# One-core fused block: output product over rounded halves from the third batch, first layer norm by aggregations

## The chip, the cores and the metric

The kernel runs on one core of a Trainium2 chip. The metric is device time in microseconds (us) of one execution. The time before is 390.41 us, the median of 3 runs (390.02 to 390.94).

## The reference

16 batches of a 512 x 256 activation pass through a state-space layer and a channel mixer, each behind a modulated layer norm. Cut to what matters:

```
h = layernorm(x) * (1 + ca) + sa
u, gate = split(h @ W_in.T)
decay = exp(-min(softplus(u @ W_dt.T + b_dt), 10) * rate)
state[t] = decay[t] * state[t-1] + (1 - decay[t]) * (u @ W_state.T)[t]
z = (state @ W_C.T) * silu(gate) + h * D
x1 = x + ga * (z @ W_out.T)              # the output product
h2 = layernorm(x1) * (1 + cb) + sb
xr, xk = mixes of h2 and h2 one token earlier
x2 = x1 + gb * sigmoid(xr @ W_r) * (relu(xk @ W_k)^2 @ W_v)
```

## The kernel before, in words

Every engine has a hand-written list of instructions, one block of code for each engine, and all of them loop over the same STEPS (20 of them, s = 0 to 19). In step s four batches are at work: a = s (first layer norm), b = s-1 (state-space layer and output product), c = s-2 (second layer norm and the mixes), d = s-3 (channel mixer and output). Nothing reorders the instructions: what stands late in an engine's list waits for what stands before it, and semaphores tie the lists together.

Channels lie on the partitions, in 2 halves of 128, and the 512 tokens of a batch along the free axis, so a tile `x[:, i]` is 128 x 512. Most products are done in float32r over rounded halves: ScalarE (ACT) copies x into `x_hi` (rounded), GpSimd (POOL) subtracts it to get `x_lo` (helper `low_part`, L665), and TensorE (PE) multiplies `x_hi` by `w_hi` and `w_lo` and `x_lo` by `w_hi`. That is so for `h` (front and gate products), `xk`, `xr` and `k_act`. Two products are in plain float32: `state` with `w_y` (L320), and the output product, `z` with `w_late` at OUT. `half` (L207) issues the matmuls of one input half: two, one for each output half.

The end of a PE step reads: second norm's transposes, `k_hi` products, transposes of `xn1`, `k_lo` half 0, `z` half 0, `k_lo` half 1, `z` half 1 (which raises `o_ps`). The next step opens with the K product, `xk_hi` half 0 with `wl_hi` and `wl_lo`, and waits for `xk_hi`, both `xk` and both `xr`. Then come `xk_hi` half 1, four `h_hi` products, `xk_lo` half 0, four `h_hi`, `xk_lo` half 1, two `h_lo`, and the transposes of `x1` (L290).

ACT ends a step with `r_gate` (tanh, L465) and four `prev` (L392), and opens the next with `xk_hi` half 0 (L400), `h` (L407), `xk_hi` half 1 (L410), `h` (L412), `h_hi` (L415). VectorE (DVE) computes `z` (L604), the mixes `xk`, `xr`, `xr`, `xk` (L550; the second pair waits for the fourth `prev`), the first norm's statistics two batches ahead (L489), the gated value (L624), the first norm's `mean_variance` (five operations on 128 x 4, L496 to L505), `x2` (L631), `x1` (L637, waits for `o_ps`). `x1` reads the output product from PSUM, and the second norm and the residual need it. POOL runs `xk_lo` twice, `h_lo` twice, `xr_lo`, `rstd2` (L698), `prev`'s first column, `xr_lo`, the first norm's scale (`ln1_scale`, L672 and L674), `k_lo` twice.

Of the kernel before, what the change touches and what calls it, by code (L numbers as in the profile page):

```python
# [26 lines left out]
def adaln_block(nc, x_tok_d, x_ch_d, w_d, wmod_d, c_d, cols_d, ident_d, out_d):  # L27
# [6 lines left out]
    with ExitStack() as ctx:  # L34
        def sb(name, shape, dt=F32):
            return ctx.enter_context(nc.sbuf_tensor(name, shape, dt))

        def sem(name):
            return ctx.enter_context(nc.semaphore(name))

        def sems(name, n=CH):
            return [sem(f"{name}{i}") for i in range(n)]
# [9 lines left out]
        w_front = sb("w_front", [P, CH, 2 * NS])  # L52
        wf_hi = sb("wf_hi", [P, CH, 2 * NS + C], F32R)
        wf_lo = sb("wf_lo", [P, CH, 2 * NS + C], F32R)
        wl_hi = sb("wl_hi", [P, CH, 3 * C], F32R)
        wl_lo = sb("wl_lo", [P, CH, 3 * C], F32R)
        ident = sb("ident", [P, P])
        cols = sb("cols", [P, 8])
        c_sb = sb("c_sb", [P, CH * NB])
# [16 lines left out]
        x_ch = sb("x_ch", [P, 2, CH, T])  # L76
        x1 = sb("x1", [P, 3, CH, T])
        stats1 = sb("stats1", [P, 2, TT, 6])
        mv1 = sb("mv1", [P, 2, 5, TT])
        rstd1 = sb("rstd1", [P, 2, TT])  # L80
        shift1 = sb("shift1", [P, 2, TT])
        xn1 = sb("xn1", [P, TT, C])
# [50 lines left out]

        xn1a_ok, h_ok, hhi_ok, e_ok, l_ok, decay_ok = sem("xn1a_ok"), sem("h_ok"), sem("hhi_ok"), sem("e_ok"), sem("l_ok"), sem("decay_ok")
        silu_ok, tanh_ok, khi_ok, relu_ok, kact_ok = sem("silu_ok"), sem("tanh_ok"), sem("khi_ok"), sem("relu_ok"), sem("kact_ok")
        prev_ok, xkhi_ok, xrhi_ok = sems("prev_ok"), sems("xkhi_ok"), sems("xrhi_ok")

        st1_ok, halves1_ok, spread1_ok, mv1_ok, xn1b_ok = sem("st1_ok"), sem("halves1_ok"), sem("spread1_ok"), sem("mv1_ok"), sem("xn1b_ok")
        st2_ok, halves2_ok, spread2_ok, mv2_ok = sem("st2_ok"), sem("halves2_ok"), sem("spread2_ok"), sem("mv2_ok")
        xn2a_ok, xn2b_ok = sem("xn2a_ok"), sem("xn2b_ok")  # L140
        clip_ok, drive_ok, state_ok, yg_ok, rv_ok = sem("clip_ok"), sem("drive_ok"), sem("state_ok"), sem("yg_ok"), sem("rv_ok")
        z_ok, x1_ok, xk_ok, xr_ok, x2_ok = sems("z_ok"), sems("x1_ok"), sems("xk_ok"), sems("xr_ok"), sems("x2_ok")

        rstd1_ok, shift1_ok, rstd2_ok, first_ok = sem("rstd1_ok"), sem("shift1_ok"), sem("rstd2_ok"), sem("first_ok")
        hlo_ok, xklo_ok, xrlo_ok, klo_ok = sems("hlo_ok"), sems("xklo_ok"), sems("xrlo_ok"), sems("klo_ok")

        def col(j):
            return cols[:, j:j + 1]
# [54 lines left out]
        def _(pe):  # L203
# [43 lines left out]
            for s in STEPS:  # L247
                a, b, c, d = s, s - 1, s - 2, s - 3
                if live(d):
                    if d == 0:  # L250
                        pe.wait_ge(wl_lo_ok, 3)
                    pe.wait_ge(xkhi_ok[0], d + 1)
                    for x_done in (*xk_ok, *xr_ok):
                        pe.wait_ge(x_done, d + 1)
                    half(k_out, wl_hi, MIX_K, xk_hi, 0, first=True)
                    half(k_out, wl_lo, MIX_K, xk_hi, 0)
                if live(d):
                    pe.wait_ge(xkhi_ok[1], d + 1)
# [118 lines left out]

        @block.scalar
        def _(act):
# [14 lines left out]

            for s in STEPS:
                a, b, c, d = s, s - 1, s - 2, s - 3
                if live(d):
                    act.wait_ge(xk_ok[0], d + 1)
                    before(act, k_ps, d)
                    nc.scalar.copy(xk_hi[:, 0], xk[:, 0]).then_inc(xkhi_ok[0], 1)  # L400
# [56 lines left out]
                if b == 0:  # L457
                    act.wait_ge(s_wl, 16)
                    for at in (MIX_K, MIX_R, MIX_V):
                        nc.scalar.copy(wl_hi[:, :, at:at + C], w_late[:, :, at:at + C]).then_inc(wl_hi_ok, 1)  # L460
                if live(d):
                    nc.scalar.activation(k_act[:], k_act[:], ACT.Square).then_inc(kact_ok, 1)  # L462
                    act.wait_ge(r_ps, d + 1)
                    before(act, rv_ok, d)
                    nc.scalar.activation(r_gate[:], ps_r[:], ACT.Tanh, scale=0.5).then_inc(tanh_ok, 1)  # L465
                if live(c):
                    if c == 0:
                        act.wait_ge(mix_ok, 1)
                    act.wait_ge(t3_ps, c + 1)
                    before(act, xk_ok[0], c)  # L470
                    previous(KEY, 0, c)
                    before(act, xr_ok[0], c)
                    previous(REC, 0, c).then_inc(prev_ok[0], 1)
                    before(act, xr_ok[1], c)
                    previous(REC, 1, c)
                    before(act, xk_ok[1], c)
                    previous(KEY, 1, c).then_inc(prev_ok[1], 1)

        @block.vector
        def _(dve):  # L480
# [8 lines left out]
                    last = nc.vector.bn_stats(st[:, t, :], x[:, t, :])  # L489
                last.then_inc(st_ok, 1)  # L490

            def mean_variance(st, mv, st_ok, halves_ok, spread_ok, mv_ok, k, negative=False):
# [6 lines left out]
                if negative:  # L499
                    nc.vector.scalar_tensor_tensor(mv[:, 0, :], mv[:, 2, :], 0.5, st[:, :, 1], ALU.mult, ALU.subtract)  # L500
                else:
                    nc.vector.scalar_tensor_tensor(mv[:, 0, :], mv[:, 2, :], -0.5, st[:, :, 1], ALU.mult, ALU.add)
# [79 lines left out]
            for s in STEPS:  # L582
# [78 lines left out]
        def _(pool):  # L661
# [22 lines left out]
            for s in STEPS:  # L684
# [64 lines left out]
```

## Time and profile before

| | before |
|---|---|
| time, median of 3 | 390.41 us (390.02 to 390.94) |
| the profiled execution's own time | 390.1 us |
| its span | 388.3 us, granted TensorE clock 0.996 |
| PE busy | 369.3 us (95%) |
| weight loads (PEld) busy | 265.3 us (68%) |
| DVE busy | 317.1 us (82%) |
| ACT busy | 288.6 us (74%) |
| POOL busy | 201.8 us (52%) |

Times are us from the span's start. A row of a timeline reads: start, duration (of the group, where x2 or more stand at its end), engine, line, operation, tiles, and in brackets the idle time before it and what ended it. A float32 matmul of 128 x 512 shows as two matmul records with a weight load each, a float32r one as one. PEld is the weight load, which runs ahead of its matmul. POOL's queue and the DMAs keep up; neither stands in the way in the stretches discussed.

### The profile page before, as it was taken

The page shows a single profiled execution, that of the slowest core. Times are in us where ns is not written, and L with a number is a line of the kernel's source. Part 1 is how long each engine was busy: PE and PEld are TensorE (multiplying, and loading weights), DVE is VectorE, ACT ScalarE, POOL GpSimd, SP SyncE. Part 2 cuts the span into 40 slices and gives each one's busy share as a digit, 9 for nine tenths or more (in the row PEclk, how much of TensorE's full clock was granted, in tenths as well). Part 3 has the DMA queues.
Part 4 walks back from the last instruction along what each step waited for, and adds up shares of the span by engine and source line. Part 5 has one row for each costly group of instructions (what it writes and reads, how often), then busy time and mean ns, then how long its engine had stood idle before and what let it go on. Part 6 is the DMA issues. An engine that isn't in the chain of part 4 may idle for free.

```text
span 388.3 us, 5293 instructions
## 1 busy us (share of the span) xinstructions
PE 369.3 (95%) x1624; PEld 265.3 (68%) x1627; DVE 317.1 (82%) x653; ACT 288.6 (74%) x375; POOL 201.8 (52%) x198
## 2 busy tenths in 40 slices
PE   8998899999999999999999999999999999999773
PEld 4766487676777677676767767676767767676651
DVE  3787987989889797988979798888979787768552
ACT  4467678687887878689687868888787878967471
POOL 2053355666364556656454566645455663635552
PEclk9999999999999999999999999999999999999998
DMA  8921111130403131040313113040302020000111
GB/s 283 394 77 54 54 57 54 56 110 0 164 0 108 55 104 60 12 152 0 118 47 108 56 56 107 3 159 3 111 0 87 24 92 17 23 32 0 57 54 54
DMA packets 18604, 29.13 MB, mean 75 GB/s; under 512 B 1168, under 2 KB 9616, under 8 KB 18448
## 3 DMA queue, kind: packets, MB, share of 16 engines
q1 hardware_dynamic: 18144, 28.71, 21.4%
q8 instruction: 13, 0.21, 0.2%
q10 hardware_dynamic: 432, 0.09, 0.1%
q14 instruction: 15, 0.12, 0.1%
HBM read 20.40 MB, written 8.39 MB: 74 GB/s over the span
## 4 chain that ended last, share of the span: by engine, by line
issue 49%; POOL 37%; PE 7%; DVE 3%; ACT 2%; POOLq 1%; DVEq 0%; ACTq 0%
POOL xr_lo L665 10%; POOL xk_lo L665 10%; POOL k_lo L665 6%; POOL h_lo L665 5%; POOL rstd L672 3%; PE slot L207 2%; PE slot L228 2%; PE slot L221 1%; DVE stats L489 1%; PE slot L320 1%; POOLq L24 1%; POOL prev L703 1%; PE slot L214 1%; ACT prev L392 1%; DVE state L587 1%
## 5 line engine op out<-in xcount | busy, mean ns | idle before, releaser
L665 POOL TENSOR_TENSOR xk_lo<-xk,xk_hi 128x512 fp32r<-128x512 f32 x32 | 40.9, 1279 | 52.7 <-ACT xk_hi L400 47.1
L207 PE MATMUL slot<-z,w_in 128*128 128x512 f32 x128 | 59.8, 592 | 0.0
L698 POOL TENSOR_TENSOR rstd<-mv,half_neg 128x4 f32<-128x4 f32 x16 | 16.1, 1007 | 76.5 <-DVE mv L505 76.5
L665 POOL TENSOR_TENSOR k_lo<-k_act,k_hi 128x512 fp32r<-128x512 f32 x32 | 40.6, 1291 | 20.7 <-ACT k_act L462 20.7
L392 ACT ACTIVATE prev<-slot,mod,mix_prev 128x512 f32<-128x512 f32 x64 | 44.5, 784 | 2.8 <-PE slot L214 2.8
L207 PE MATMUL slot<-h_hi,wf_hi 128*128 128x512 f32 x128 | 46.0, 400 | 0.4 <-ACT h_hi L415 0.4
L207 PE MATMUL slot<-h_hi,wf_lo 128*128 128x512 f32 x128 | 45.1, 393 | 0.0
L665 POOL TENSOR_TENSOR h_lo<-h,h_hi 128x512 fp32r<-128x512 f32 x30 | 38.3, 1298 | 9.6 <-ACT h_hi L415 9.6
L427 ACT ACTIVATE dt<-slot,cols 128x512 f32<-128x512 f32 x16 | 11.0, 688 | 41.5 <-PE slot L207 41.5
L665 POOL TENSOR_TENSOR xr_lo<-xr,xr_hi 128x512 fp32r<-128x512 f32 x32 | 41.5, 1299 | 0.0
L550 DVE SCALAR_TENSOR_TENSOR xk<-slot,mix_new,prev 128x512 f32<-128x512 f32 x32 | 23.9, 747 | 18.8 <-issue 18.8
L214 PE MATMUL slot<-ident,xn 128*128 128x128 f32 x256 | 35.7, 273 | 2.8 <-DVE xn L526 2.1
L207 PE MATMUL slot<-h_lo,wf_hi 128*128 128x512 f32 x128 | 37.4, 395 | 0.0
L214 PEld LDWEIGHTS slot<-ident,xn 128*128 128x128 f32 x256 | 30.4, 140 | 10.1 <-DVE xn L526 2.8
L207 PEld LDWEIGHTS slot<-z,w_in 128*128 128x128 f32 x128 | 24.0, 189 | 18.8 <-issue 16.3
L320 PE MATMUL slot<-state,w_in 128*128 128x512 f32 x64 | 30.2, 594 | 2.5 <-DVE state L587 2.5
L526 DVE TENSOR_SCALAR xn<-slot,mv,rstd 128x256 f32<-128x256 f32 x64 | 30.1, 534 | 1.1 <-POOL rstd L698 1.1
L599 DVE TENSOR_TENSOR slot<-silu,slot 128x1024 f32<-128x1024 f32 x16 | 19.7, 1229 | 13.5 <-PE slot L320 13.5
L465 ACT ACTIVATE r_gate<-slot 128x1024 f32<-128x1024 f32 x16 | 16.4, 1028 | 18.6 <-PE slot L207 18.6
L207 PEld LDWEIGHTS slot<-h_hi,wf_hi 128*128 128x128 f32 x128 | 24.0, 188 | 6.7 <-issue 0.9
L207 PE MATMUL slot<-xk_hi,wl_hi 128*128 128x512 f32 x64 | 26.2, 491 | 2.2 <-DVE xk L550 2.2
L207 PEld LDWEIGHTS slot<-h_hi,wf_lo 128*128 128x128 f32 x128 | 24.2, 189 | 5.9 <-issue 0.2
(99 smaller groups left out, 900.4 us busy)
## 6 DMA issues: line engine op xcount, KB each, us to landing
x_tok<-x_tok_in SPq DMA_DIRECT2D x16, 512.0 KB, 3.5
x_ch<-x_ch_in SPq DMA_DIRECT2D x16, 512.0 KB, 3.9
x_out<-wmod SPq DMA_DIRECT2D x15, 512.0 KB, 3.0
wmod<-wmod_in SPq DMA_DIRECT2D x1, 1024.0 KB, 10.1
w_in<-weights_in SPq DMA_DIRECT2D x1, 1024.0 KB, 11.5
w_in<-weights_in SPq DMA_DIRECT2D x1, 768.0 KB, 5.5
wmod<-wmod_in SPq DMA_DIRECT2D x1, 512.0 KB, 6.4
x_out<-wmod SPq DMA_DIRECT2D x2, 256.0 KB, 2.2
```

Of the source, the lines that this page charges most:

```text
L207: ins = nc.tensor.matmul(out, w[:, c, at + d * P:at + (d + 1) * P], x[:, c, :], start=first, stop=last)
L214: last = nc.tensor.transpose(out[:, c, t * P:(t + 1) * P], x[:, t, c * P:(c + 1) * P], ident[:])
L320: last = nc.tensor.matmul(ps_y[:, i, :], w_y[:, i * P:(i + 1) * P], state[:], start=True, stop=True)
L392: return nc.scalar.activation(prev[:, mix, i, 1:T + 1], ps_n[:, i, :], ACT.Identity, bias=mod_at(SHIFT2 + i, k), scale=mix_prev[:, mix, i, ...
L427: nc.scalar.activation(dt[:], ps_front[:, 0, :], ACT.Exp, bias=col(B_DT)).then_inc(e_ok, 1)
L465: nc.scalar.activation(r_gate[:], ps_r[:], ACT.Tanh, scale=0.5).then_inc(tanh_ok, 1)
L526: last = nc.vector.tensor_scalar(xn2[:, t, :], ps_x1[:, t, :], mv2[:, k % 2, 0, t:t + 1], rstd2[:, k % 2, t:t + 1], ALU.subtract, ALU.mult)
L550: nc.vector.scalar_tensor_tensor(x[:, i, :], ps_n[:, i, :], mix_now[:, mix, i, k:k + 1], prev[:, mix, i, 0:T], ALU.mult, ALU.add).then_inc ...
L599: nc.vector.tensor_tensor(ps_y[:], silu[:], ps_y[:], ALU.mult).then_inc(yg_ok, 1)
L665: nc.gpsimd.tensor_tensor(lo, x, hi.bitcast(F32), ALU.subtract).then_inc(done, 1)
L672: nc.gpsimd.tensor_tensor(rstd1[:, k % 2], mv1[:, k % 2, 1, :], half_neg[:], ALU.pow).then_inc(rstd1_ok, 1)
L698: nc.gpsimd.tensor_tensor(rstd2[:, c % 2], mv2[:, c % 2, 1, :], half_neg[:], ALU.pow).then_inc(rstd2_ok, 1)
```

## The change

The output product of batches 2 to 15 (`split(k)`) goes over rounded halves: ACT copies z into z_hi (half 0 between the second and the third `prev`, half 1 at the head of the next step), POOL makes z_lo after `k_lo`, and PE multiplies z_hi by the halves of W_out where z stood, and z_lo inside the K product of the next step, which is where `o_ps` is raised now. Batches 0 and 1 stay in float32. ACT and POOL split W_out once, in step 2. The first norm's mean and variance are made by one aggregation per token tile, four in all, and POOL negates the mean and adds epsilon.

```diff
+        WHOLE = 2
+        def split(k):
+            return WHOLE <= k < NB
 # PE, head of a step
                     half(k_out, wl_hi, MIX_K, xk_hi, 0, first=True)
                     half(k_out, wl_lo, MIX_K, xk_hi, 0)
+                if split(c):
+                    pe.wait_ge(zlo_ok[0], c - WHOLE + 1)
+                    half(o_out, wl_hi, OUT, z_lo, 0)
                 if live(d):
                     pe.wait_ge(xkhi_ok[1], d + 1)
                     half(k_out, wl_hi, MIX_K, xk_hi, 1)
                     half(k_out, wl_lo, MIX_K, xk_hi, 1)
+                if split(c):
+                    pe.wait_ge(zlo_ok[1], c - WHOLE + 1)
+                    half(o_out, wl_hi, OUT, z_lo, 1, last=True).then_inc(o_ps, 1)
 # PE, end of a step
-                    pe.wait_ge(z_ok[0], b + 1)
                     before(pe, tanh_ok, d + 1 if live(d) else 0)
-                    half(o_out, w_late, OUT, z, 0, first=True)
+                    if split(b):
...
+                        pe.wait_ge(zhi_ok[0], b - WHOLE + 1)
+                        half(o_out, wl_hi, OUT, z_hi, 0, first=True)
+                        half(o_out, wl_lo, OUT, z_hi, 0)
+                    else:
+                        pe.wait_ge(z_ok[0], b + 1)
+                        half(o_out, w_late, OUT, z, 0, first=True)
                 if live(d):
                     pe.wait_ge(klo_ok[1], d + 1)
                     half(v_out, wl_hi, MIX_V, k_lo, 1, last=True).then_inc(v_ps, 1)
-                if live(b):
+                if split(b):
+                    pe.wait_ge(zhi_ok[1], b - WHOLE + 1)
+                    half(o_out, wl_hi, OUT, z_hi, 1)
+                    half(o_out, wl_lo, OUT, z_hi, 1)
+                elif live(b):
                     pe.wait_ge(z_ok[1], b + 1)
                     half(o_out, w_late, OUT, z, 1, last=True).then_inc(o_ps, 1)
 # ACT
+                if split(c):
+                    act.wait_ge(z_ok[1], c + 1)
+                    nc.scalar.copy(z_hi[:, 1], z[:, 1]).then_inc(zhi_ok[1], 1)
...
+                if b == 1:
+                    nc.scalar.copy(wl_hi[:, :, OUT:OUT + C], w_late[:, :, OUT:OUT + C]).then_inc(wl_hi_ok, 1)
...
                     previous(REC, 0, c).then_inc(prev_ok[0], 1)
+                if split(b):
+                    act.wait_ge(z_ok[0], b + 1)
+                    before(act, o_ps, b)
+                    nc.scalar.copy(z_hi[:, 0], z[:, 0]).then_inc(zhi_ok[0], 1)
+                if live(c):
                     before(act, xr_ok[1], c)
                     previous(REC, 1, c)
 # DVE
-                mean_variance(stats1[:, k % 2], mv1[:, k % 2], st1_ok, halves1_ok, spread1_ok, mv1_ok, k, negative=True)
+                dve.wait_ge(st1_ok, k + 1)
+                for t in range(TT):
+                    last = nc.vector.bn_aggr(mv1[:, k % 2, t, :], stats1[:, k % 2, t, :])
+                last.then_inc(mv1_ok, 1)
...
-                        before(dve, o_ps, b)
+                        if split(b - 1):
+                            dve.wait_ge(zlo_ok[i], b - WHOLE)
+                        else:
+                            before(dve, o_ps, b)
 # POOL
-                nc.gpsimd.tensor_tensor(rstd1[:, k % 2], mv1[:, k % 2, 1, :], half_neg[:], ALU.pow).then_inc(rstd1_ok, 1)
+                nc.gpsimd.tensor_scalar(spread1[:, k % 2, 0, :], mv1[:, k % 2, :, 0], -1.0, None, ALU.mult)
+                nc.gpsimd.tensor_scalar(spread1[:, k % 2, 1, :], mv1[:, k % 2, :, 1], EPS, None, ALU.add).then_inc(spread1_ok, 1)
+                pool.wait_ge(spread1_ok, k + 1)
+                nc.gpsimd.tensor_tensor(rstd1[:, k % 2], spread1[:, k % 2, 1, :], half_neg[:], ALU.pow).then_inc(rstd1_ok, 1)
...
+                if split(b):
+                    for i in range(CH):
+                        pool.wait_ge(zhi_ok[i], b - WHOLE + 1)
+                        pool.wait_ge(o_ps, b)
+                        nc.gpsimd.tensor_tensor(z_lo[:, i], z[:, i], z_hi[:, i].bitcast(F32), ALU.subtract).then_inc(zlo_ok[i], 1)
```

Line numbers in the changed kernel are higher (L207 is L216 there). On PE, at the turn of a step, before:

```order
L207 MATMUL slot<-k_lo,wl_hi 128x512 x2
L207 MATMUL slot<-z,w_in 128x512 x2
L207 MATMUL slot<-xk_hi,wl_hi 128x512 x2
L207 MATMUL slot<-xk_hi,wl_lo 128x512 x2
L207 MATMUL slot<-xk_hi,wl_hi 128x512 x2
L207 MATMUL slot<-xk_hi,wl_lo 128x512 x2
L207 MATMUL slot<-h_hi,wf_hi 128x512
```

The same place in the changed kernel:

```order
L216 MATMUL slot<-k_lo,wl_hi 128x512 x2
L216 MATMUL slot<-z_hi,wl_hi 128x512 x2
L216 MATMUL slot<-z_hi,wl_lo 128x512 x2
L216 MATMUL slot<-xk_hi,wl_hi 128x512 x2
L216 MATMUL slot<-xk_hi,wl_lo 128x512 x2
L216 MATMUL slot<-z_lo,wl_hi 128x512 x2
L216 MATMUL slot<-xk_hi,wl_hi 128x512 x2
L216 MATMUL slot<-xk_hi,wl_lo 128x512 x2
L216 MATMUL slot<-z_lo,wl_hi 128x512 x2
L216 MATMUL slot<-h_hi,wf_hi 128x512
```

Two float32 matmuls per half became four float32r ones, and two more per half moved into the K product.

On ACT at the same turn, in the changed kernel (before, the four `prev` stood together and `xk_hi` came right after them):

```order
L496 ACTIVATE r_gate<-slot 128x1024
L418 ACTIVATE prev<-slot,mod,mix_prev 128x512 x2
L508 CAST z_hi<-z 128x512
L418 ACTIVATE prev<-slot,mod,mix_prev 128x512 x2
L425 CAST z_hi<-z 128x512
L429 CAST xk_hi<-xk 128x512
L436 ACTIVATE h<-slot,mod 128x512
L439 CAST xk_hi<-xk 128x512
```

One copy stands ahead of the third and fourth `prev`, the other ahead of `xk_hi`, `h` and `h_hi`.

## Rows read from the trace of the kernel before

**Rows 1.** Timeline, PE: first K matmuls of steps 14, 15 and 16.

```profile
292.69 1.03 PE L207 MATMUL slot<-xk_hi,wl_hi 128*128 128x512 f32 x2
...
314.94 1.03 PE L207 MATMUL slot<-xk_hi,wl_hi 128*128 128x512 f32 x2
...
336.69 1.03 PE L207 MATMUL slot<-xk_hi,wl_hi 128*128 128x512 f32 x2
```

**Rows 2.** Waits: engine line <- releaser: us in total, times, longest.

```profile
PE slot L290 <- DVE x L637: 3.2, 11, 0.3
```

**Rows 3.** Timeline, weight loads at the turn of a step.

```profile
199.94 0.42 PEld L207 LDWEIGHTS slot<-z,w_in 128*128 128x128 f32 x2
...
203.65 0.19 PEld L207 LDWEIGHTS slot<-xk_hi,wl_hi 128*128 128x128 f32 x1 [0.24 <-issue]
...
205.71 0.19 PEld L207 LDWEIGHTS slot<-h_hi,wf_hi 128*128 128x128 f32 x1
...
208.50 0.42 PEld L207 LDWEIGHTS slot<-h_lo,wf_hi 128*128 128x128 f32 x2
```

**Rows 4.** Timeline, DVE and POOL: the first norm's small operations, x2, x1.

```profile
204.24 0.16 DVE L496 TENSOR_TENSOR mv<-stats 128x4 f32<-128x4 f32 x1
...
204.39 2.56 POOL L665 TENSOR_TENSOR h_lo<-h,h_hi 128x512 fp32r<-128x512 f32 x2 [0.48 <-ACT h_hi L415]
204.52 1.19 DVE L500 SCALAR_TENSOR_TENSOR mv<-mv,stats 128x4 f32<-128x4 f32 x1
...
206.89 1.40 DVE L631 SCALAR_TENSOR_TENSOR wmod<-slot,mod,x 128x512 f32<-128x512 f32 x2
...
208.21 1.39 DVE L637 SCALAR_TENSOR_TENSOR x<-slot,mod,x_ch 128x512 f32<-128x512 f32 x2
```

**Rows 5.** Timeline, ACT: head of one step, end of it and head of the next.

```profile
200.29 0.64 ACT L400 CAST xk_hi<-xk 128x512 fp32r<-128x512 f32 x1
200.80 0.81 ACT L407 ACTIVATE h<-slot,mod 128x512 f32<-128x512 f32 x1
...
201.94 0.62 ACT L410 CAST xk_hi<-xk 128x512 fp32r<-128x512 f32 x1 [0.32 <-DVE xk L550]
...
203.26 1.05 ACT L415 CAST h_hi<-h 128x1024 fp32r<-128x1024 f32 x1
...
209.40 0.69 ACT L427 ACTIVATE dt<-slot,cols 128x512 f32<-128x512 f32 x1 [2.64 <-PE slot L207]
...
218.98 1.03 ACT L465 ACTIVATE r_gate<-slot 128x1024 f32<-128x1024 f32 x1 [1.11 <-PE slot L207]
...
219.90 2.78 ACT L392 ACTIVATE prev<-slot,mod,mix_prev 128x512 f32<-128x512 f32 x4
...
222.55 0.64 ACT L400 CAST xk_hi<-xk 128x512 fp32r<-128x512 f32 x1
```

**Rows 6.** Timeline, DVE: the mixes of that step.

```profile
221.44 0.75 DVE L550 SCALAR_TENSOR_TENSOR xk<-slot,mix_new,prev 128x512 f32<-128x512 f32 x1 [1.15 <-issue]
...
222.10 1.40 DVE L550 SCALAR_TENSOR_TENSOR xr<-slot,mix_new,prev 128x512 f32<-128x512 f32 x2
...
223.42 0.74 DVE L550 SCALAR_TENSOR_TENSOR xk<-slot,mix_new,prev 128x512 f32<-128x512 f32 x1
```

**Rows 7.** Timeline, steps 16 to 18: prev, x1's transposes, last waits on xn and xk.

```profile
352.41 2.78 ACT L392 ACTIVATE prev<-slot,mod,mix_prev 128x512 f32<-128x512 f32 x4
...
360.62 0.95 PEld L290 LDWEIGHTS slot<-ident,x 128*128 128x128 f32 x8
...
366.26 0.66 PE L214 MATMUL slot<-ident,xn 128*128 128x128 f32 x4 [2.11 <-DVE xn L526]
...
371.87 0.74 DVE L550 SCALAR_TENSOR_TENSOR xk<-slot,mix_new,prev 128x512 f32<-128x512 f32 x1
...
372.79 0.30 PEld L207 LDWEIGHTS slot<-xk_hi,wl_hi 128*128 128x128 f32 x2 [2.61 <-issue]
```

**Rows 8.** Timeline, POOL in step 0: the first norm's shift.

```profile
8.08 0.20 POOL L674 TENSOR_TENSOR shift<-mv,rstd 128x4 f32<-128x4 f32 x1
```

More of the change, by code:

```diff
@@ L54, in adaln_block @@
         wf_lo = sb("wf_lo", [P, CH, 2 * NS + C], F32R)
-        wl_hi = sb("wl_hi", [P, CH, 3 * C], F32R)
-        wl_lo = sb("wl_lo", [P, CH, 3 * C], F32R)
+        wl_hi = sb("wl_hi", [P, CH, 4 * C], F32R)
+        wl_lo = sb("wl_lo", [P, CH, 4 * C], F32R)
         ident = sb("ident", [P, P])
@@ L78, in adaln_block @@
         stats1 = sb("stats1", [P, 2, TT, 6])
-        mv1 = sb("mv1", [P, 2, 5, TT])
+        mv1 = sb("mv1", [P, 2, TT, 2])
+        spread1 = sb("spread1", [P, 2, 2, TT])
         rstd1 = sb("rstd1", [P, 2, TT])
@@ L94, in adaln_block @@
         z = sb("z", [P, CH, T])
+        z_hi = sb("z_hi", [P, CH, T], F32R)
+        z_lo = sb("z_lo", [P, CH, T], F32R)
         prev = sb("prev", [P, 2, CH, T + 1])
@@ L135, in adaln_block @@
         silu_ok, tanh_ok, khi_ok, relu_ok, kact_ok = sem("silu_ok"), sem("tanh_ok"), sem("khi_ok"), sem("relu_ok"), sem("kact_ok")
-        prev_ok, xkhi_ok, xrhi_ok = sems("prev_ok"), sems("xkhi_ok"), sems("xrhi_ok")
-        st1_ok, halves1_ok, spread1_ok, mv1_ok, xn1b_ok = sem("st1_ok"), sem("halves1_ok"), sem("spread1_ok"), sem("mv1_ok"), sem("xn1b_ok")
+        zhi_ok, prev_ok, xkhi_ok, xrhi_ok = sems("zhi_ok"), sems("prev_ok"), sems("xkhi_ok"), sems("xrhi_ok")
+        st1_ok, mv1_ok, xn1b_ok = sem("st1_ok"), sem("mv1_ok"), sem("xn1b_ok")
         st2_ok, halves2_ok, spread2_ok, mv2_ok = sem("st2_ok"), sem("halves2_ok"), sem("spread2_ok"), sem("mv2_ok")
@@ L142, in adaln_block @@
         z_ok, x1_ok, xk_ok, xr_ok, x2_ok = sems("z_ok"), sems("x1_ok"), sems("xk_ok"), sems("xr_ok"), sems("x2_ok")
-        rstd1_ok, shift1_ok, rstd2_ok, first_ok = sem("rstd1_ok"), sem("shift1_ok"), sem("rstd2_ok"), sem("first_ok")
-        hlo_ok, xklo_ok, xrlo_ok, klo_ok = sems("hlo_ok"), sems("xklo_ok"), sems("xrlo_ok"), sems("klo_ok")
+        spread1_ok, rstd1_ok, shift1_ok, rstd2_ok, first_ok = sem("spread1_ok"), sem("rstd1_ok"), sem("shift1_ok"), sem("rstd2_ok"), sem("first_ok")
+        hlo_ok, zlo_ok, xklo_ok, xrlo_ok, klo_ok = sems("hlo_ok"), sems("zlo_ok"), sems("xklo_ok"), sems("xrlo_ok"), sems("klo_ok")
         def col(j):
@@ L367, in _ @@
                         pe.wait_ge(s_wl, 16)
-                    pe.wait_ge(z_ok[0], b + 1)
                     before(pe, tanh_ok, d + 1 if live(d) else 0)
-                    half(o_out, w_late, OUT, z, 0, first=True)
+                    if split(b):
+                        if b == WHOLE:
+                            pe.wait_ge(wl_lo_ok, 4)
+                        pe.wait_ge(zhi_ok[0], b - WHOLE + 1)
[4 more added lines that the diff above has]
+                        half(o_out, w_late, OUT, z, 0, first=True)
                 if live(d):
@@ L490, in statistics, with mean_variance @@
                 last.then_inc(st_ok, 1)
-            def mean_variance(st, mv, st_ok, halves_ok, spread_ok, mv_ok, k, negative=False):
+            def mean_variance(st, mv, st_ok, halves_ok, spread_ok, mv_ok, k):
                 dve.wait_ge(st_ok, k + 1)
@@ L498, in mean_variance @@
                 dve.wait_ge(halves_ok, k + 1)
[L499 to L502, printed above, removed]
+                nc.vector.scalar_tensor_tensor(mv[:, 0, :], mv[:, 2, :], -0.5, st[:, :, 1], ALU.mult, ALU.add)
                 nc.vector.scalar_tensor_tensor(mv[:, 4, :], mv[:, 2, :], 0.25, mv[:, 2, :], ALU.mult, ALU.mult).then_inc(spread_ok, 1)
@@ L671, in ln1_scale @@
                 before(pool, xn1b_ok, k - 1)
-                nc.gpsimd.tensor_tensor(rstd1[:, k % 2], mv1[:, k % 2, 1, :], half_neg[:], ALU.pow).then_inc(rstd1_ok, 1)
+                nc.gpsimd.tensor_scalar(spread1[:, k % 2, 0, :], mv1[:, k % 2, :, 0], -1.0, None, ALU.mult)
+                nc.gpsimd.tensor_scalar(spread1[:, k % 2, 1, :], mv1[:, k % 2, :, 1], EPS, None, ALU.add).then_inc(spread1_ok, 1)
+                pool.wait_ge(spread1_ok, k + 1)
+                nc.gpsimd.tensor_tensor(rstd1[:, k % 2], spread1[:, k % 2, 1, :], half_neg[:], ALU.pow).then_inc(rstd1_ok, 1)
                 pool.wait_ge(rstd1_ok, k + 1)
-                nc.gpsimd.tensor_tensor(shift1[:, k % 2], mv1[:, k % 2, 0, :], rstd1[:, k % 2], ALU.mult).then_inc(shift1_ok, 1)
+                nc.gpsimd.tensor_tensor(shift1[:, k % 2], spread1[:, k % 2, 0, :], rstd1[:, k % 2], ALU.mult).then_inc(shift1_ok, 1)
             def weight_low_part(n, at):
@@ L713, in _ @@
                         weight_low_part(n, at)
+                if b == 1:
+                    weight_low_part(4, OUT)
 def kernel(**inputs):
```

## The prediction

> **What bounds the kernel now.** I read the page first: PE is busy 95% of the span, the others far less, so what counts is PE's list and the few places where it waits. The chain that ended last runs mostly through "issue" and POOL and says little here; the timeline of PE says more. The first K matmuls of steps 14, 15 and 16 stand 22.25 and 21.75 us apart [rows 1]. The two intervals hold the same matmuls; the longer one has a wait of x1's transposes for DVE, which occurs 11 times [rows 2]. The row counts 0.29 us of idleness, but the step is 0.50 us longer: the following loads have lost their lead too. So a step is 21.75 us of pure matmul issue, plus 0.50 in 11 steps. ACT waits for PE before r_gate, 1.11 us [rows 5], and catches up with it every step: a step can be reckoned from r_gate's start to r_gate's start.
>
> Below, times lie in the turn after 218.98; a row from the turn before it is moved by 222.55 - 200.29 = 22.26 us [rows 5].
>
> **PE's work.** A float32 record takes 0.19 + 0.24 = 0.43 us from load to load; in float32r the 12 loads from 205.71 to 208.50 take 0.2325 each [rows 3]. Before, a batch has 8 records (3.44 us); now 12 (2.79). Saved: **0.65 us per batch**, 14 batches. Where the matmul itself is 4 passes to 1, by the Trainium skill's FP8 and Floating Point Precision (TensorE Precision Notes: true FP32 takes four passes through the array), the three products would be 3/4 of 3.44, 2.58, and 0.86 saved. The trace gives the float32r matmul 0.2325 and not 3.44 / 16 = 0.215, and the sum goes by the trace.
>
> **x1's wait.** DVE's first-norm block takes 206.89 - 204.24 = 2.65 us for five operations on 4 columns, since some last 1.19 while POOL runs h_lo [rows 4] and 0.16 otherwise. Four aggregations take its place. No row shows one; the nearest are these: 0.16 with starts 0.08 apart for 4 columns would make 0.4 for the group, four statistics of 256 columns (some 0.35 each) 1.4 at most. I take 0.5, as an aggregation reads 6 columns. x1 ends now 7.71 us after the last xk (from 224.16, which is rows 6, to 208.21 + 1.39 + 22.26 = 231.87); new 7.71 - 2.65 + 0.5 = 5.56 after it. If this beats PE, 11 x 0.50 = **5.5 us** go.
>
> **The new wait, at the K product.** Each of ACT's copies pushes what follows by 0.51 (200.29 to 200.80 [rows 5]). The prevs start 0.665 apart. So z_hi half 0 starts at 221.23, the fourth prev at 222.41 and ends at 223.19. DVE's second xr follows by 0.09 (as 221.44 follows the second prev's end), xk by 0.66, and it ends at 224.68, 0.52 later than now [rows 5, 6]. PE's load follows by 0.18 (372.61 to 372.79 [rows 7]): 224.86. PE would be free for it sooner: first z load 199.94 + 22.26 = 222.20 [rows 3], plus 10 loads of 0.2325, 224.52. It is 0.34 late; after a wait the second load comes 0.30 - 0.19 = 0.11 behind the first [rows 7], which gives 0.12 back. **Loss 0.22 us per turn.** z_hi half 1 ends at 223.69, its load free at 223.59: also late, and covered by the K wait.
>
> Next in line, all from the K load at 224.86:
> - h_hi: ACT's second copy and the later xk_hi move it to an end at 227.13; PE asks for it at 224.86 - 0.12 + 12 x 0.2325 = 227.53. Slack 0.40.
> - POOL has two more subtractions of 1.28 in front of xk_lo and h_lo. z_lo half 1 starts at 223.79, xk_lo end at 227.6, h_lo at 230.1; PE asks at 227.53 + 2.79 = 230.32. **Slack 0.2**, the thinnest.
> - x1: 224.68 + 5.56 = 230.24, o_ps long there (about 228.1); PE asks at 230.32 + 0.465 = 230.79. Slack 0.5; the aggregations may cost up to 1.0.
>
> xr_hi and the table load fall into ACT's 2.6 us wait for dt. POOL's small additions in ln1_scale (2 x 0.20 by the shift's row [rows 8], and a semaphore) lie one step ahead of their use; in step 0 they may cost 0 to 0.5, less what the shorter aggregation gives; I take 0. The split of W_out in step 2 meets idle ACT and POOL.
>
> **The tail.** In step 16 no xn1 transposes stand ahead of z. With prev at 352.41 [rows 7] the same steps give xk's end at 357.21, K load 357.39, z_lo half 1 last load 359.83. What reads a product starts some 0.67 after its last load (208.73, the second of the pair in rows 3, to 209.40 [rows 5]), so o_ps releases x1 at 360.5; it ends at 361.9. Transposes start at 361.95, not 360.62 [rows 7]. PE later idles 2.11 for xn, which comes from x1: the whole **1.33 us** is lost.
>
> **Sum** against the profiled 390.1: 13 turns up to r_gate of step 16 gain 13 x (0.65 - 0.22) = 5.6; x1's waits 5.5; tail -1.3. 390.1 - 9.8 = 380.3. The median lies 0.3 above the profiled run: **380.5 us**, 2.5% faster.
>
> **Rivals.**
> - **PE loses nothing at the turn** (10%). ACT's copy hides in some gap or xk comes sooner: +13 x 0.22 = 2.9 more, 377.6. If float32r cost 0.215 here by the page's four passes, it would be 0.86 per batch, 13 x 0.21 = 2.7 more, also 377.8. Rows 3 speak against the second, the strict order of ACT's list against the first.
> - **h_lo comes late** (15%). POOL's slack is 0.2; 0.3 to 0.5 more on its path (waits between five subtractions in a row, a tail of the copies) costs PE 0.1 to 0.3 a turn: 381.8 to 384.4.
> - **x1 still late** (15%). If the four aggregations take 1.5, PE waits as now: 5.5 lost, 386.0.
> - **The aggregations are held behind POOL** (5%, slower). What holds the small operations is seen: 1.19 against 0.16 under h_lo [rows 4]. The Trainium skill's SBUF - State Buffer (Who interferes with whom) says that a VectorE instruction with at most one SBUF input, outside the two-port modes, does not contend with GpSimd, one with two does; no run here shows it for an aggregation. By that rule an aggregation runs free, and the forecast stands. If instead each of three waited a subtraction of 1.28 out, the group takes 3.8 instead of 0.5, x1 comes 3.3 - 0.5 = 2.8 after PE asks, and each of the 11 turns costs 2.8 more than forecast: 380.5 + 31 = 411. It decides from a group of 1.0 on (first wait), and turns the sign at about 1.9 (9.9 us of gain given back over 11 turns). That two small operations under h_lo went by after one wait speaks against a train of them.
>
> **How the numbers follow.** Forecast 55%, rivals 10, 15, 15 and 5. Range 377.0 to 387.0: it takes in the first three rivals and +-0.1 us per turn on ACT's copies (+-1.3), and leaves out the last. A measurement here can tell 0.2%, 0.8 us. Faster 0.93, same 0.02, slower 0.05.
>
> **What would show it.** K matmuls 21.3 us apart in steps 4 to 16; the last xk ending 5.7 after r_gate's start (5.2 now) and the K load right behind it; no wait of L305's transposes for x1; L548's four in 0.3 to 0.6 with no jump while POOL runs; h_lo's end just ahead of its matmul; z_hi and z_lo records at 0.23. The prediction is wrong if K matmuls still stand 21.7 or more apart, if PE waits for POOL's h_lo or z_lo, or if the tail after step 16 grows by 3 us.

## The result and the profile after

380.17 us, the median of 4 runs (379.41 to 380.68), against 390.43 for the kernel before beside it: ratio 0.9735, interval 0.9713 to 0.9757. The forecast was 380.5. The profiled execution has a span of 377.9 us (388.3 before).

The profile page's busy times of the changed kernel (share of the span, instructions):

```profile
PE 362.0 (96%) x1680; PEld 275.4 (73%) x1683; DVE 301.9 (80%) x637; ACT 300.9 (80%) x404; POOL 247.3 (65%) x259
```

PE lost 7 us of busy time, DVE 15; ACT took on 12 and POOL 45. PE stays the bound. ACT's timeline gives the turn, here the time from one r_gate's start to the next:

```profile
190.29 1.03 ACT L496 ACTIVATE r_gate<-slot 128x1024 f32<-128x1024 f32 x1 [1.00 <-PE slot L216]
...
211.59 1.03 ACT L496 ACTIVATE r_gate<-slot 128x1024 f32<-128x1024 f32 x1 [1.00 <-PE slot L216]
```

21.30 us, where it was 22.26 [rows 5], and 21.32 follows from the prediction (21.75 - 0.65 + 0.22). The same turn of the changed kernel in the timeline of all engines:

```profile
193.04 1.46 ACT L418 ACTIVATE prev<-slot,mod,mix_prev 128x512 f32<-128x512 f32 x2
...
194.54 0.75 DVE L586 SCALAR_TENSOR_TENSOR xr<-slot,mix_new,prev 128x512 f32<-128x512 f32 x1 [0.39 <-ACT prev L418]
...
195.07 0.30 PEld L216 LDWEIGHTS slot<-z_hi,wl_hi 128*128 128x128 f32 x2 [0.21 <-ACT z_hi L425]
...
195.21 0.74 DVE L586 SCALAR_TENSOR_TENSOR xk<-slot,mix_new,prev 128x512 f32<-128x512 f32 x1
...
196.13 0.30 PEld L216 LDWEIGHTS slot<-xk_hi,wl_hi 128*128 128x128 f32 x2 [0.30 <-issue]
...
198.30 0.37 DVE L548 BATCH_NORM_AGGREGATE mv<-stats 128x2 f32<-128x6 f32 x4
...
198.80 0.19 PEld L216 LDWEIGHTS slot<-h_hi,wf_hi 128*128 128x128 f32 x1
...
198.86 2.54 POOL L704 TENSOR_TENSOR h_lo<-h,h_hi 128x512 fp32r<-128x512 f32 x2
...
199.88 1.40 DVE L676 SCALAR_TENSOR_TENSOR x<-slot,mod,x_ch 128x512 f32<-128x512 f32 x2
...
201.61 0.42 PEld L216 LDWEIGHTS slot<-h_lo,wf_hi 128*128 128x128 f32 x2
202.07 1.03 PEld L305 LDWEIGHTS slot<-ident,x 128*128 128x128 f32 x8
```

- **The new wait** stands where it was put: DVE's second xr waits 0.39 for the fourth prev, which stands behind ACT's copy. The last xk ends at 195.95, 5.66 after r_gate (5.70 forecast, 5.18 before [rows 5, 6]), and the K load follows at 196.13, after 0.30 of idleness. ("issue" in that row means that the profile names no releaser; that it is the xk is read from the times, and filling the gap shows it below.)
- **x1's wait** is gone in all 11 steps. The aggregations take 0.37 as a group while POOL subtracts, against 2.65 before [rows 4]. x1 ends at 201.28, 0.79 ahead of its transposes' load.
- **h_lo** ends at 201.40, its matmul's load comes at 201.61: the slack of 0.2.

The sum by places, read at r_gate's start. The 13 turns from step 3 to step 16 took 351.49 - 63.16 = 288.33 us before and 339.45 - 62.46 = 276.99 after: 11.3 gained, 11.1 forecast. The first r_gate in it, before and after:

```profile
63.16 1.03 ACT L465 ACTIVATE r_gate<-slot 128x1024 f32<-128x1024 f32 x1 [0.96 <-PE slot L207]
```

```profile
62.46 1.03 ACT L496 ACTIVATE r_gate<-slot 128x1024 f32<-128x1024 f32 x1 [1.00 <-PE slot L216]
```

In step 16 the transposes of x1 come late, by the timeline of the changed kernel:

```profile
339.45 1.03 ACT L496 ACTIVATE r_gate<-slot 128x1024 f32<-128x1024 f32 x1 [1.11 <-PE slot L216]
...
349.89 0.86 PEld L305 LDWEIGHTS slot<-ident,x 128*128 128x128 f32 x8 [1.01 <-DVE x L676]
...
357.07 1.02 ACT L496 ACTIVATE r_gate<-slot 128x1024 f32<-128x1024 f32 x1 [4.65 <-PE slot L216]
```

10.44 us after r_gate, 9.13 before [rows 7]: 1.31 lost, 1.33 forecast. Two things were not forecast. The stretch from x1's transposes to the next r_gate is 0.4 longer, on which more at the end. And the first three steps are 0.7 shorter, by the waits of PE for the state product (us in total, times, longest), before and after:

```profile
PE slot L320 <- DVE state L587: 2.5, 2, 1.8
```

```profile
PE slot L335 <- DVE state L623: 1.7, 2, 1.4
```

One of the two falls from 0.71 to 0.34, the other from 1.75 to 1.38. The total is 1.7 us in every kernel here with aggregations and 2.5 in the two variants below that keep the small operations, wherever they stand. So this gain comes with the aggregations and not with the split.

### The profile page after: what moved, and what is told of

It is laid out like the page before. It is cut to its first block, busy times and chain, and to the rows that moved or that the text cites. A ratio compares the mean times of both kernels' runs of the same rounds, so it can differ in the third digit from the quotient of the medians.

```text
span 377.9 us, 5521 instructions
## 1 busy us (share of the span) xinstructions
PE 362.0 (96%) x1680; PEld 275.4 (73%) x1683; DVE 301.9 (80%) x637; ACT 300.9 (80%) x404; POOL 247.3 (65%) x259
## 4 chain that ended last, share of the span: by engine, by line
issue 43%; POOL 43%; PE 5%; DVE 3%; ACT 2%; DMA 1%; POOLq 1%; DVEq 0%; SPq 0%; ACTq 0%
POOL xr_lo L704 11%; POOL z_lo L757 7%; POOL k_lo L704 6%; POOL xk_lo L704 6%; POOL h_lo L704 6%; POOL rstd L714 3%; PE slot L216 2%; DMA w_in<-weights_in 1%; PE slot L230 1%; PE slot L335 1%; DVE stats L525 1%; POOL prev L745 1%; POOL spread L712 1%; POOL spread L711 1%; PE slot L223 1%
## 5 line engine op out<-in xcount | busy, mean ns | idle before, releaser
L757 POOL TENSOR_TENSOR z_lo<-z,z_hi 128x512 fp32r<-128x512 f32 x28 | 36.3, 1296 | 26.5 <-ACT z_hi L508 18.7
L418 ACT ACTIVATE prev<-slot,mod,mix_prev 128x512 f32<-128x512 f32 x64 | 46.3, 785 | 2.0 <-PE slot L223 2.0
L216 PE MATMUL slot<-h_hi,wf_hi 128*128 128x512 f32 x128 | 45.9, 399 | 0.4 <-ACT h_hi L444 0.4
L216 PE MATMUL slot<-h_hi,wf_lo 128*128 128x512 f32 x128 | 45.7, 398 | 0.0
L704 POOL TENSOR_TENSOR xr_lo<-xr,xr_hi 128x512 fp32r<-128x512 f32 x32 | 42.5, 1330 | 0.0
L216 PE MATMUL slot<-h_lo,wf_hi 128*128 128x512 f32 x128 | 37.6, 396 | 0.0
L216 PEld LDWEIGHTS slot<-h_hi,wf_hi 128*128 128x128 f32 x128 | 24.1, 188 | 6.9 <-issue 0.9
L216 PEld LDWEIGHTS slot<-h_hi,wf_lo 128*128 128x128 f32 x128 | 24.1, 188 | 6.1 <-issue 0.2
L216 PEld LDWEIGHTS slot<-h_lo,wf_hi 128*128 128x128 f32 x128 | 24.0, 188 | 5.9 <-issue 0.4
L586 DVE SCALAR_TENSOR_TENSOR xr<-slot,mix_new,prev 128x512 f32<-128x512 f32 x32 | 23.7, 746 | 5.5 <-ACT prev L418 5.5
```

The lines of the kernel that those rows point to most:

```text
L216: ins = nc.tensor.matmul(out, w[:, c, at + d * P:at + (d + 1) * P], x[:, c, :], start=first, stop=last)
L418: return nc.scalar.activation(prev[:, mix, i, 1:T + 1], ps_n[:, i, :], ACT.Identity, bias=mod_at(SHIFT2 + i, k), scale=mix_prev[:, mix, i, ...
L586: nc.vector.scalar_tensor_tensor(x[:, i, :], ps_n[:, i, :], mix_now[:, mix, i, k:k + 1], prev[:, mix, i, 0:T], ALU.mult, ALU.add).then_inc ...
L704: nc.gpsimd.tensor_tensor(lo, x, hi.bitcast(F32), ALU.subtract).then_inc(done, 1)
L757: nc.gpsimd.tensor_tensor(z_lo[:, i], z[:, i], z_hi[:, i].bitcast(F32), ALU.subtract).then_inc(zlo_ok[i], 1)
```

## The experiments

### One half of the change alone

The kernel before with the four aggregations and POOL's three lines for them, nothing else.

```diff
-                mean_variance(stats1[:, k % 2], mv1[:, k % 2], st1_ok, halves1_ok, spread1_ok, mv1_ok, k, negative=True)
+                dve.wait_ge(st1_ok, k + 1)
+                for t in range(TT):
+                    last = nc.vector.bn_aggr(mv1[:, k % 2, t, :], stats1[:, k % 2, t, :])
+                last.then_inc(mv1_ok, 1)
```

> The kernel before with the first norm's four aggregations alone, the output product all float32. Theory (the five small operations held behind POOL make x1 late, and each of 11 late x1 costs PE 0.50 us): K matmuls stand 21.75 us apart in steps 4 to 14 too, no wait of the x1 transposes, 390.4 - 5.5 = 384.9. Rival (the idle time of the row, 0.29 us, is all that such a wait costs): 390.4 - 3.2 = 387.2. Rival (the aggregations are held behind POOL like the operations they replace): 390.4.

Measured: 384.29 us (384.14 to 384.67), ratio 0.9834 (0.9818 to 0.985). Turns of 21.75 throughout, no wait of x1's transposes. (The gain is 6.5 by the medians and 5.8 by the spans of the two profiled executions, 388.3 and 382.5; the turns hold 5.5 of it.) The first rival, the idleness of the row taken for the price, and the second both fall.

The other half: the changed kernel with the five small operations put back.

> The changed kernel with the first norm's five small operations as before; only the output product is split. Theory (the two halves of the change lean on each other: the split brings PE to x1's transposes 1.4 us earlier in the turn and DVE's xk 0.5 later, so the small operations, held behind POOL's subtractions, make x1 late by about 2 us in 11 steps): 380.2 + 22 = about 402, slower than before, K matmuls 23.3 apart. Rival (the parts add up, each worth what it is worth alone): 380.2 + 5.5 = 385.7.

Measured: 406.94 us, the median of three executions (404.94 to 410.2), ratio 1.0423 (1.037 to 1.0476); a fourth took 418.03 at a mean granted clock of 0.962. So the split alone makes the kernel 4% slower, and the parts don't add up: by the ratios -6.5 and +16.5 us give -10.3 together. The timeline of this variant (POOL's second xk_lo runs from 192.53 on, then both h_lo, and xr_lo from 196.29):

```profile
193.22 0.62 DVE L532 TENSOR_TENSOR mv<-stats 128x4 f32<-128x4 f32 x1
...
193.76 1.32 DVE L533 SCALAR_TENSOR_TENSOR mv<-stats 128x4 f32<-128x4 f32 x1
193.78 2.55 POOL L704 TENSOR_TENSOR h_lo<-h,h_hi 128x512 fp32r<-128x512 f32 x2
...
195.12 1.23 DVE L536 SCALAR_TENSOR_TENSOR mv<-mv,stats 128x4 f32<-128x4 f32 x1
...
196.28 1.31 DVE L539 SCALAR_TENSOR_TENSOR mv<-mv 128x4 f32<-128x4 f32 x1
...
197.62 0.16 DVE L541 SCALAR_TENSOR_TENSOR mv<-mv 128x4 f32<-128x4 f32 x1
...
200.49 1.09 PE L305 MATMUL slot<-ident,x 128*128 128x128 f32 x8 [3.11 <-DVE x L676]
```

Four of five operations on four columns last as long as what is left of a POOL subtraction: each of them ends within 0.03 us of the end of one. PE stands still for 3.11 us; in the other eight turns three are held, and it is 1.5 to 1.7. Turns of the second kind take 23.17 (23.3 expected). Those of the first kind take 26.2: more than the wait, for the granted clock falls behind it. The view by stretches of this variant (length; busy time and instructions of PE, PEld, DVE, ACT, POOL; granted clock, 1.00 being the level of 2.4 GHz; DMA) shows the turn around the wait:

```profile
195.00:200.50 5.50, 2.39 (x12) 1.59 (x10) 5.43 (x9) 2.45 (x4) 2.57 (x3) 1.00 0.09 33
200.50:205.50 5.00, 5.00 (x19) 4.13 (x20) 4.50 (x14) 3.98 (x6) 1.56 (x3) 0.66 0.55 179
205.50:211.00 5.50, 5.50 (x24) 3.83 (x23) 3.18 (x6) 2.67 (x3) 2.67 (x4) 1.00 0.28 95
```

A mean of 0.66 over 5 us is some 3.4 us at the lower level, 1.2 GHz. Three turns of the profiled run had it, which the expectation of 402 had not counted: each took 3.0 us more than the others, 1.4 by the longer wait and 1.7 by the clock (3.4 us at half speed).

### Is it the place or the number of the small operations?

```diff
-                if live(a + 2) and a > 1:
-                    ln1_mean_variance(a + 2)
...
                 if live(a + 1) and a > 0:
                     ln1_apply(a + 1)
+                if live(a + 2) and a > 1:
+                    ln1_mean_variance(a + 2)
```

> The kernel before, its five small operations of the first norm kept but moved behind x1 and the application of the norm in DVE's list, where POOL stands idle. Theory (it is their place beside POOL's h_lo that costs, not their number): they last 0.16 each, x1 comes in time, turns of 21.75, 384.9 as with the aggregations. Rival (DVE's load as such, or the kind of operation, makes x1 late): 387 to 390.4.

Measured: 384.45 us (384.39 to 384.53), ratio 0.9853 (0.9837 to 0.987), turns of 21.75. In the rows of this variant's tile mv the operation that lasted 1.18 in the median (L500) now lasts (shortest, median, longest in ns):

```profile
L500 DVE SCALAR_TENSOR_TENSOR mv<-mv,stats x16: 164/166/167, 6.4 to 292.7; 128x4 f32<-128x4 f32 x16
```

Moving two lines gives what the aggregations give in the turns. Another kind of operation was not needed, the place beside POOL's subtractions was the fault.

### How long may the aggregations take?

In both variants further aggregations, into a buffer that nobody reads, stand ahead of the four: 4 of them, and 28 in the second.

```diff
+                for t in range(4 if k > 3 else 0):
+                    nc.vector.bn_aggr(dump[:, k - 4, t, :], stats1[:, k % 2, t % TT, :])
```

> The changed kernel with eight aggregations in place of four in 12 steps, four of them into a buffer that nobody reads. Theory (an aggregation costs 0.073 behind another and is not held by POOL; x1 has 0.74 us of slack): group of 0.66, 380.2, no wait of x1's transposes. Rival (every DVE instruction beside POOL runs a risk of being held for up to 1.3): over 382.

> The same with 32 aggregations. Theory: the group lasts 0.15 + 31 x 0.073 = 2.4, 2.0 more than now, x1 comes 1.3 late, which costs about 1.5 of a turn with the lost lead: 12 x 1.5 = 18, 398. Rival (held behind POOL): 401 and more, with aggregations of over 1 us among the rows.

Measured: 379.07 us with eight (378.9 to 379.55, ratio 0.9717, 0.9703 to 0.9732), turns of 21.29, no cost (it lies 1.1 below the changed kernel; half of that is in step 16 to 17, where the clock plays in, below); 389.88 us with 32 (389.21 to 391.26, ratio 0.9993, 0.9982 to 1.0003). The theory holds in kind: none of the 336 further aggregations was held (143 to 181 ns each), though POOL ran beside them. In size it missed by 8 us. The timeline with 32:

```profile
204.06 1.95 DVE L549 BATCH_NORM_AGGREGATE dump<-stats 128x2 f32<-128x6 f32 x28
204.61 2.56 POOL L707 TENSOR_TENSOR h_lo<-h,h_hi 128x512 fp32r<-128x512 f32 x2
...
208.94 1.09 PE L306 MATMUL slot<-ident,x 128*128 128x128 f32 x8 [0.74 <-DVE x L679]
```

The turn is 22.25, 0.95 longer than the changed kernel's. PE's row says 0.74. In the kernel before it said 0.29 and the turn was 0.50 longer [rows 1, 2]; in the split alone 1.68 and 1.87. **The price of a wait is PE's idle time plus 0.2**, and it is less than the lateness of the load (here x1 ends 1.1 after the load would have started), because loads run ahead of their matmuls. That is how I read the difference; the three pairs show the sum, not the mechanism. I had taken the lateness and added the lost lead once more. The group lasts 2.3 here, and the kernel is as fast as the one before: the prediction had the sign turn at 1.9.

### The wait at the K product

One more ACT copy behind z_hi half 0:

```diff
                     nc.scalar.copy(z_hi[:, 0], z[:, 0]).then_inc(zhi_ok[0], 1)
+                    nc.scalar.copy(spare[:], z[:, 0])
```

> The changed kernel with one more ACT copy of 128 x 512 right after z_hi half 0, into a buffer that nobody reads. Theory (the last xk sets the K product, by ACT's list): each of 14 turns is 0.51 later, 380.2 + 7.1 = 387.3, the last xk ends 6.2 after the start of r_gate. Rival (ACT has room at this place and the K wait is set by PE's own list): 380.2 to 381.

Measured: 387.47 us (386.73 to 387.51), ratio 0.991 (0.9893 to 0.9927). The turn is 215.50 - 193.68 = 21.82 against 21.30: each 0.51 us of ACT at this place is paid in full. DVE's xr waits 0.91 now. One reading differs: what grew on PE is the wait for z_hi half 1, from 0.21 of the load's idle time to 0.72, while that of the K load stays at 0.31:

```profile
198.45 0.75 DVE L588 SCALAR_TENSOR_TENSOR xr<-slot,mix_new,prev 128x512 f32<-128x512 f32 x1 [0.91 <-ACT prev L419]
...
198.97 0.19 PEld L217 LDWEIGHTS slot<-z_hi,wl_hi 128*128 128x128 f32 x1 [0.72 <-ACT z_hi L426]
```

So the copy delays two things that stand close together, the last xk and z_hi half 1, and this run can't tell which of them is paid for. The next two can: they give PE something to do while it waits, the z_lo half 0 matmuls, once ahead of the K product, once a place earlier, ahead of z_hi half 1.

```diff
+                if split(c):
+                    pe.wait_ge(zlo_ok[0], c - WHOLE + 1)
+                    half(o_out, wl_hi, OUT, z_lo, 0)
                 if live(d):
...
                     half(k_out, wl_hi, MIX_K, xk_hi, 0, first=True)
                     half(k_out, wl_lo, MIX_K, xk_hi, 0)
-                if split(c):
-                    pe.wait_ge(zlo_ok[0], c - WHOLE + 1)
-                    half(o_out, wl_hi, OUT, z_lo, 0)
```

> The changed kernel with the two z_lo half 0 matmuls moved ahead of the K product's first matmuls: same matmuls, other order. Theory (K waits 0.3 us for xk in each turn, 0.22 of it lost; z_lo half 0 is ready by then and fills the gap): the wait at K is gone, the h_hi load comes 0.14 earlier, 13 turns x 0.14 = 1.8 us, 378.4; the slack of h_lo falls from 0.21 to 0.07. Rival (h_lo's path through POOL is the true bound and takes over at once): 379.5 to 380.2, with a wait of PE for POOL's h_lo in the rows.

Measured: 378.63 us (377.86 to 379.48), ratio 0.9694 (0.9673 to 0.9715).

```diff
                 if split(b):
+                    pe.wait_ge(zlo_ok[0], b - WHOLE + 1)
+                    half(o_out, wl_hi, OUT, z_lo, 0)
                     pe.wait_ge(zhi_ok[1], b - WHOLE + 1)
                     half(o_out, wl_hi, OUT, z_hi, 1)
```

> The changed kernel with the two z_lo half 0 matmuls one place earlier still, ahead of z_hi half 1: they fill the wait for z_hi half 1 (0.21 of idle time in the rows) and, by the same lead, the one for xk. Theory (PE's own list is what is left after it): turns of 21.10, 13 x 0.20 = 2.6 us less than the changed kernel, 377.6. Rival (POOL's chain z_lo, xk_lo twice, h_lo twice starts at z_hi half 1 and its slack of 0.21 in the changed kernel is used up at 0.07 in the variant before): the turn stays at 21.15 to 21.18, 378.3 to 378.6, with PE waiting for h_lo.

Measured: 376.67 us (376.59 to 377.07), ratio 0.9655 (0.9641 to 0.9668). The turns in order, from ACT's timeline: first variant

```profile
189.79 1.03 ACT L496 ACTIVATE r_gate<-slot 128x1024 f32<-128x1024 f32 x1 [0.99 <-PE slot L216]
...
210.99 1.03 ACT L496 ACTIVATE r_gate<-slot 128x1024 f32<-128x1024 f32 x1 [1.00 <-PE slot L216]
```

and second:

```profile
189.35 1.03 ACT L495 ACTIVATE r_gate<-slot 128x1024 f32<-128x1024 f32 x1 [1.00 <-PE slot L216]
...
210.48 1.03 ACT L495 ACTIVATE r_gate<-slot 128x1024 f32<-128x1024 f32 x1 [0.99 <-PE slot L216]
```

As means over 13 turns: 21.31 for the changed kernel, 21.18 and 21.14. The wait at K was worth 0.13 of a turn, the one for z_hi half 1 another 0.04. Both expectations took 21.10 for the pure list and POOL's h_lo for the rival. In the second variant, with loads 0.2325 apart, PE would load for h_lo at 200.51; h_lo ends at 200.48 in POOL (197.92 + 2.56), and the load comes at 200.60, 0.09 late. The matmuls don't feel it:

```profile
197.92 2.56 POOL L703 TENSOR_TENSOR h_lo<-h,h_hi 128x512 fp32r<-128x512 f32 x2
...
200.27 0.63 PE L216 MATMUL slot<-xk_lo,wl_hi 128*128 128x512 f32 x2
...
200.60 0.33 PEld L216 LDWEIGHTS slot<-h_lo,wf_hi 128*128 128x128 f32 x2
...
200.74 0.63 PE L216 MATMUL slot<-h_lo,wf_hi 128*128 128x512 f32 x2
...
201.21 1.04 PE L302 MATMUL slot<-ident,x 128*128 128x128 f32 x8
```

The pairs start 0.47 apart, 200.27, 200.74 and 201.21, the pace of two matmuls without a wait, and it is so in all 13 turns. So the rival is out here too, and 21.14 is the pure list: the split takes 0.62 off PE's list of 21.75 (282.79 and 274.77 us over 13 turns), and not 0.65.

The second variant is 2.0 us faster than the first, by the medians, where the turns give 0.5. The step from r_gate of step 16 to the next takes 16.65 in place of 17.54. Of these 0.9 us, x1 coming earlier in the tail makes 0.35 (its transposes 9.94 after r_gate of step 16, 10.29 in the first). In the rest the clock plays in: between PE's wait for xn and that r_gate the first variant has a mean granted clock of 0.61, the second 0.99.

### The tail, and all together

```diff
-            return WHOLE <= k < NB
+            return WHOLE <= k < NB - 1
```

> The changed kernel with the last batch's output product in float32 again (batches 2 to 14 split). Theory (in step 16 the product's last part and two ACT copies stand ahead of x1, and the chain to the end hangs on x1: 1.3 us): 380.2 - 1.3 = 378.9, x1's transposes 9.1 after the start of r_gate of step 16 and not 10.4. Rival (the tail hangs on something else, PE's own list): 380.2.

Measured: 378.30 us (377.9 to 378.97), ratio 0.9696 (0.9683 to 0.9709). The transposes of x1 come 9.13 after r_gate of step 16 (348.63 - 339.50), to the hundredth as before the change: the last batch was better left whole.

With this, batch 1 split as well (WHOLE = 1, its low part of W_out ahead of z_lo in POOL's list) and z_lo half 0 at the one or the other place:

> z_lo half 0 ahead of the K product, the last batch in float32, and batch 1 split too (its W_out low part made ahead of z_lo). Theory (the three are at different places and add up): 378.6 - 1.3 - 0.4 = 376.9. Rival (step 2 has no room for batch 1's halves, since W_out's low part and the pow of the norms stand in POOL's list): 377.3 or more.

> As the one before, with z_lo half 0 ahead of z_hi half 1 instead. Theory (PE's list left): 0.8 less than it, 376.1. Rival (h_lo through POOL is the bound): equal to it within 0.3.

Measured: 376.01 us (375.74 to 376.34, ratio 0.9636, 0.9623 to 0.9649) and 375.40 us (375.25 to 376.2, ratio 0.9624, 0.9611 to 0.9637). The second is the fastest here, 3.8% under the kernel before and, by the two ratios, 1.1% under the change. Its intervals overlap with the first's: 0.6 of the expected 0.8 is seen and not certain. The first lies 0.9 below its expectation of 376.9: its way from r_gate of step 16 to the next takes 15.91, as in the kernel before (15.93), where the changed kernel with the last batch whole takes 16.31 at a lower clock.

## Why the prediction was right

Point by point, by its own steps.

- **PE's work, 0.65 us per batch.** A little too large: 0.62, by the turns of 21.75 with the aggregations alone and 21.14 with both gaps filled. The matmuls of z_hi and z_lo stand 0.23 apart in the rows after. The 0.86 that four passes against one would give is out. The trace neither bears out nor refutes the count of passes of the Trainium skill's FP8 and Floating Point Precision (TensorE Precision Notes): in time a float32 matmul costs 3.7 float32r ones here. Each float32r matmul has its load beside it, at 0.2325 and not 0.215; whether the load is the reason is not shown.
- **x1's wait, 0.50 in 11 steps.** Right: the aggregations alone took 6.5 us off, the move of the small operations 5.7, and the turns hold 5.5 of each. The group took 0.37 for 0.5, the slack was 0.79 for 0.5.
- **The rule on the shared side of SBUF.** The Trainium skill's SBUF - State Buffer (Who interferes with whom) lets a VectorE instruction with at most one SBUF input, outside the two-port modes, run free of GpSimd, and one with two contend with it. The traces agree on both: 336 and 64 aggregations at 143 to 182 ns beside POOL, the held two-input operations up to 1.33. No run changed the number of inputs alone, so that it is the inputs that decide is not shown here apart from the Trainium skill. The slower rival went by the opposite and is out. But it named a real danger at the wrong instruction: with the small operations left in, the split alone is 16 us slower than the kernel before. And its argument against a train of waits misread the rows: under h_lo one small operation went by after a wait, the next waited again, as the kernel before shows behind the 1.19 of [rows 4]:

```profile
205.63 0.15 DVE L503 SCALAR_TENSOR_TENSOR mv<-mv 128x4 f32<-128x4 f32 x1
...
205.82 1.15 DVE L505 SCALAR_TENSOR_TENSOR mv<-mv 128x4 f32<-128x4 f32 x1
```
- **The wait at K.** The times of ACT's copies, the last xk and the K load came within 0.05 us of the forecast. Its weight was the weak term: 0.22 per turn forecast, 0.17 measured, 0.13 at K and 0.04 at z_hi half 1, which the prediction had taken as covered. This and the 0.03 too much in PE's work cancel: 21.75 - 0.62 + 0.17 gives the same turn as 21.75 - 0.65 + 0.22. That 21.30 met 21.32 so closely is in part luck.
- **The slack of h_lo, 0.2.** As forecast. Where the changed order uses it up, h_lo's load comes late and PE's matmuls still do not.
- **The tail, 1.33.** 1.31 at x1's transposes, shown again by leaving the last batch whole. The 0.4 behind it is the clock's, below.
- **The balance.** 13 turns gave 11.3 for 11.1, the tail took 1.7 for 1.3, the start gave 0.7 for 0. The last is the term that the prediction put at nothing: it set POOL's additions against the shorter first norm in step 0, and the shorter first norm won: PE's two waits for the state product are 0.37 shorter each. By spans 10.4 came off for 9.8. The forecast's own last step is also off by 0.1: 380.3 and 0.3 make 380.6, not 380.5.

## What to carry to other kernels

Reckon a change to a bound engine's list from one fixed point of a turn to the next, and follow each engine's list to where it must be ready: savings of one engine become waits for the next one, to the tenth of a microsecond. Small operations with two SBUF inputs on VectorE are cheap in number and dear in place: look at what GpSimd does beside them before counting them, and expect that an earlier or later neighbour moves them under it. Half of a change may be worse than nothing without the other.

## What the runs showed of the hardware

- **The clock fell behind waits of 3.1 us, and in some executions behind one of 2.1.** The split alone showed the first, in all three turns with such a wait and in none of the eight with one of 1.7 or less: 3.11 us of idleness of PE, then some 3.4 us at 1.2 GHz, and a turn of 26.2 in place of 23.2. The second shows in step 17, where PE waits 2.1 us for xn in every kernel here [rows 7]. In the changed kernel the view by stretches gives a mean of 0.72 for the 6 us behind it:

```profile
355.45:361.45 6.00, 5.92 (x22) 4.58 (x22) 2.75 (x5) 4.21 (x6) 2.82 (x4) 0.72 0.00 1
```

  In the variant with batches 1 to 14 split and z_lo half 0 ahead of the K product, where that wait ends at 352.25, the two stretches around its end have 1.00:

```profile
347.50:353.50 6.00, 3.88 (x22) 2.88 (x21) 3.96 (x13) 2.59 (x4) 3.34 (x4) 1.00 0.02 5
353.50:359.50 6.00, 3.77 (x18) 2.85 (x17) 3.63 (x5) 4.98 (x8) 2.95 (x4) 1.00 0.01 3
```

  The change had brought a wait of 0.57 for x1 some 3.4 us ahead of the other, but the fall doesn't need it: with the last batch whole that wait is gone, and the same stretch still has 0.78. The profiled execution of the kernel before stays at 1.00. Nor does the list of instructions alone decide it: over the executions of one and the same kernel the mean granted clock differs, 0.989 to 0.997 for the kernel before, 0.992 to 0.996 for the changed one. What decides it is open. In the changed kernel it costs 0.4 us up to the next r_gate, and part of it is hidden again, as PE waits 1.10 for the last xk in place of 2.20. The kernel before took 390.15 us at a mean clock of 0.990 and 390.19 at 0.997.
- **The price of a wait of PE** for x1 is its idle time in the rows plus 0.2 us: 0.29 and 0.50, 0.74 and 0.95, 1.68 and 1.87. A wait that shows as 0.3 in 11 steps is worth 5.5 us. One that shows on the loads alone, 0.30 at K, cost 0.13.
- **An operation on four columns can last 1.3 us.** The held ones have two inputs in SBUF and end within 0.03 us of the end of the subtraction that GpSimd has begun. The one right behind a held one, without a semaphore between them, mostly slips through (in the split alone it was held in 6 of 22 cases, in the kernel before in none of 11). Operations with one input in SBUF were not held: aggregations 143 to 182 ns, and in the changed kernel x1's own, which reads one tile from PSUM and one from SBUF, 737 to 754 ns in all 32.
